# A new order for the first three blocks of a conditioned sequence kernel, with one activation table set

## What is computed

```python
x = _L0_cond_ref(x, theta, phi)            # rotate channel pairs by theta and phi of the sample
# L1
h = _noise_encoding(t, E)                  # sines and cosines of 5000 * t * freqs
h = silu(h @ W1 + b1)
h = h @ W2 + b2
scale = (h @ Wsc + bsc)[:, None, :]
shift = (h @ Wsh + bsh)[:, None, :]
out = silu(scale * _layer_norm(x, gamma, beta) + shift)     # mean and variance over a whole sample
out = out @ W_in + b_in
out = silu(scale * _layer_norm(out, gamma, beta) + shift)
out = out @ W_out + b_out
x = out + x
# L2: U and V (512 x 32) are orthogonalised by Gram-Schmidt, and a steering term of rank 32 is added
# L3: a transformer block (16 heads, causal), gated per sample
```

## Time and profile before

| what | value |
|---|---|
| median of 3 runs | 1610.24 us (1608.3 to 1611.57) |
| span of the profiled execution | 1610.9 us; its own time is not given apart from the span, which is 0.66 us above the median |
| TensorE busy | 1585.8 us (98%), weight loads 1299.5 us (81%) |
| VectorE, ScalarE, GpSimd busy | 1166.6, 982.8, 410.9 us |
| DMA | 254.79 MB, 158 GB/s on average |

### The profile page before, as it was taken

One profiled execution on the slowest core, in us unless ns is written; L12 is line 12 of the kernel. 1 busy time (PEld: TensorE's weight loads), 2 busy tenths in 40 slices (PEclk: granted clock), 3 DMA queues, 4 the chain that ended last, 5 costly groups with the idle time before them and its releaser, 6 DMA issues.

```text
span 1610.9 us, 27177 instructions
## 1 busy us (share of the span) xinstructions
PE 1585.8 (98%) x9296; PEld 1299.5 (81%) x9298; DVE 1166.6 (72%) x2767; ACT 982.8 (61%) x2331; POOL 410.9 (26%) x605
## 2 busy tenths in 40 slices
PE   7999999999999999999999999999999999999999
PEld 4688786777777777777777688898999999999998
DVE  7999888786969686868778576785655656565643
ACT  6888766887878787878778755352433324242422
POOL 8998810313222313131312110201010110202010
PEclk8999999999999999999999999999999999999999
DMA  7042135543545444444337435866464555556361
GB/s 308 0 183 97 66 126 126 149 130 92 138 95 139 100 115 122 111 116 115 88 90 214 167 152 207 303 262 232 178 234 170 213 225 188 212 178 265 142 211 68
DMA packets 62257, 254.79 MB, mean 158 GB/s; under 512 B 10628, under 2 KB 16004, under 8 KB 46760
## 3 DMA queue, kind: packets, MB, share of 16 engines
q1 hardware_dynamic: 62120, 253.06, 48.2%
HBM read 153.93 MB, written 48.23 MB: 125 GB/s over the span
## 4 chain that ended last, share of the span: by engine, by line
PE 90%; POOL 3%; DMA 2%; DVE 2%; ACT 1%; issue 1%; SPq 1%; POOLq 0%; DVEq 0%; ACTq 0%
PE psum L83 24%; PE psum L84 23%; PE psum L85 23%; PE psum L1529 5%; PE psum L1549 5%; PE psum L1579 4%; PE psum L1470 1%; DMA k_weights<-w_factors 1%; PE psum L1478 1%; PE psum L2451 1%; DMA k_raw<-in_t_w 1%; POOL k_gs_square L252 1%; POOL k_gs_root L247 1%; ACT psum L1229 1%; POOL k_gs_scaled L256 1%
## 5 line engine op out<-in xcount | busy, mean ns | idle before, releaser
L1229 ACT ACTIVATE psum<-psum,b_mx 128x512 f32<-128x512 f32 (+3 forms) x512 | 258.9, 509 | 63.2 <-DVE b_mx L990 62.0
L990 DVE CUSTOM_DVE_ANT_0 psum<-psum,b_mask 128x512 f32<-128x512 f32 (+3 forms) x512 | 244.7, 506 | 53.0 <-PE psum L1529 48.1
L2398 ACT ACTIVATE k_act<-k_stack_f,k_smalls 128x512 f32<-128x512 f32 x112 | 80.9, 722 | 303.6 <-DVE k_stack_f L2237 297.1
L1241 ACT ACTIVATE k_exps<-psum 128x512 f32<-128x512 f32 (+1 forms) x384 | 194.6, 532 | 59.4 <-PE psum L1549 58.1
L864 POOL TENSOR_SCALAR_AFFINE_SELECT k_exps<-k_exps 128x256 f32<-128x256 f32 x256 | 96.4, 413 | 381.0 <-ACT k_exps L1241 379.1
L2097 POOL TENSOR_SCALAR k_result<-k_result,k_pb 128x512 f32<-128x512 f32 x32 | 59.2, 1866 | 434.9 <-DVE k_result L2156 434.9
L2216 DVE TENSOR_TENSOR k_act_lo<-k_act,k_act_hi 128x512 fp32r<-128x512 f32 x112 | 77.2, 690 | 120.6 <-ACT k_act_hi L2401 120.6
L83 PE MATMUL psum<-k_act_hi,k_w_hi 128*128 128x512 f32 x384 | 150.8, 393 | 0.0
L84 PE MATMUL psum<-k_act_lo,k_w_hi 128*128 128x512 f32 x384 | 150.5, 392 | 0.0
L85 PE MATMUL psum<-k_act_hi,k_w_lo 128*128 128x512 f32 x384 | 150.2, 391 | 0.0
L2237 DVE TENSOR_TENSOR k_raw<-psum,k_raw 128x256 f32<-128x256 f32 x168 | 70.5, 421 | 106.0 <-PE psum L85 95.4
(11 more groups left out here) (372 smaller groups left out, 4418.2 us busy)
## 6 DMA issues: line engine op xcount, KB each, us to landing
k_stack<-w_factors SPq DMA_DIRECT2D x35, 1792.0 KB, 7.7
k_stack<-k_samples SPq DMA_DIRECT2D x384, 128.0 KB, 2.4
k_weights<-w_factors SPq DMA_DIRECT2D x17, 1792.0 KB, 7.5
x<-k_tokens SPq DMA_DIRECT2D x10, 1024.0 KB, 4.3
k_tokens<-x SPq DMA_DIRECT2D x8, 1024.0 KB, 5.1
d<-k_result SPq DMA_DIRECT2D x32, 256.0 KB, 2.9
k_raw<-x SPq DMA_DIRECT2D x8, 1024.0 KB, 4.8
k_raw<-d SPq DMA_DIRECT2D x8, 1024.0 KB, 7.1
```

What stands on the lines that cost most here:

```text
L990: last = dve.tensor_tensor_reduce(got, got, mask[:, S - width:S], -INV_SQRT_DH, -2.0 * MASKED, ALU.add, ALU.min, mx[n % 2][:, h, t:t + 1])
L1229: act.activation(sc(n, u)[:, at:at + width], sc(n, u)[:, at:at + width], ACT.Exp, bias=mx[n % 2][:, h, t:t + 1], scale=-1.0, accum_out=sum ...
L1241: act.activation(exps[n % 2][:, h, at:at + width], by_key(n, u)[:, 0:width], ACT.Exp, scale=INV_SQRT_DH).then_inc(k_act, 1)
L2398: act.activation(act_f[:], whole_tile, ACT.Gelu, bias=small(smalls, "b1", 2 * pair % M + second)).then_inc(pair_gelu, 1)
```

## The change

The order of four engines' lists is changed in the opening, up to block 2, and from there on everything is as before.

- SyncE: W_in's first half is loaded behind the four weights of the modulation, gamma's and beta's first halves ahead of it, then the second halves of gamma, beta and W_in. The number of loads is the same.
- ScalarE: a new step `tables` names the set that holds both silu and sine. `weight_high(0, 0)` goes behind `squares(1)`, `weight_high(0, 1)` between the silus of block 0, the crosses of sample 2 and three of the four `bias` steps of block 0 go behind silus of block 1.
- VectorE: `hidden_biased` goes ahead of `rotate(1, 1)`; `spread`, `mean(1)`, `modulated`, `weight_low` and the `low` steps of blocks 0 and 1 change places with `centre` and `gs_step`.
- TensorE: the counts and places of `hold` change; `layer_columns(0)` comes right behind `mean(0)`; block 0 runs four openings and then four closings, where it ran three, three, one and one. Behind `opening(1, 0)` and `mean(2)` the order is the old one.
- GpSimd's list is not changed.

```diff
--- before.py
+++ after.py
@@ -464,6 +464,9 @@
                 ins = act.activation(h1[:, j, 0:B], t_bank(0)[:, j * B:(j + 1) * B], ACT.Silu, bias=small(smalls, "t_b1", j))
             ins.then_inc(mlp_act, 1)
 
+        def tables():
+            act.preload_act_table_set("silu_and_others")
+
         def rows_out(k):
             act.wait_ge(t_full, (2, 4)[k])
             act.activation(spread_out[k], t_bank(1 + k), ACT.Copy).then_inc(mlp_act, 1)
@@ -476,7 +479,7 @@
                 act.wait_ge(wout_ld, 16)
             act.activation(whole(w_hi[k])[:, at], flat(raw)[:, at], ACT.Copy).then_inc(w_hi_set, 1)
 
-        return steps(sines_out, hidden_out, rows_out, weight_high, crosses, squares, silu_high, bias)
+        return steps(tables, sines_out, hidden_out, rows_out, weight_high, crosses, squares, silu_high, bias)
 
     def tensor(pe):
         def mean(n):
@@ -2618,18 +2621,18 @@
 
     mod.gs_in()
     mod.smalls_in()
-    mod.w_in_in(0)
     mod.x_in(0)
     mod.layer_in(0)
     mod.x_in(1)
     mod.layer_in(1)
     mod.layer_in(2)
+    mod.layer_in(3)
     mod.gamma_in(0)
-    mod.layer_in(3)
+    mod.beta_in(0)
+    mod.w_in_in(0)
+    mod.gamma_in(1)
+    mod.beta_in(1)
     mod.w_in_in(1)
-    mod.gamma_in(1)
-    mod.beta_in(0)
-    mod.beta_in(1)
     mod.x_in(2)
     mod.w_out_in()
     mod.x_in(3)
@@ -2808,41 +2811,41 @@
     mod.gs_step(1)
     mod.rotate(0, 0)
     mod.rotate(0, 1)
-    mod.weight_low(0, 0)
     mod.rotate(1, 0)
     mod.mean(0)
+    mod.hidden_biased()
     mod.rotate(1, 1)
     mod.gs_step(1)
-    mod.hidden_biased()
+    mod.spread(0)
+    mod.mean(1)
     mod.centre(0, 0)
-    mod.spread(0)
     mod.shift_rows_out()
-    mod.gs_step(1)
-    mod.mean(1)
-    mod.centre(0, 1)
     mod.modulated(0)
     mod.shift(0, 0)
     mod.modulated(1)
-    mod.centre(1, 0)
+    mod.gs_step(1)
+    mod.centre(0, 1)
+    mod.weight_low(0, 0)
+    mod.spread(1)
+    mod.low(0, 0)
     mod.shift(0, 1)
     mod.weight_low(0, 1)
-    mod.spread(1)
-    mod.low(0, 0)
     mod.gs_step(1)
+    mod.centre(1, 0)
+    mod.low(0, 1)
     mod.centre(1, 1)
-    mod.low(0, 1)
     mod.shift(1, 0)
     mod.shift(1, 1)
+    mod.low(1, 0)
     mod.rotate(2, 0)
     mod.gs_step(1)
     att.row_high()
+    mod.low(1, 1)
     mod.rotate(2, 1)
-    mod.low(1, 0)
     mod.gs_step(1)
     att.row_low()
     mod.mean(2)
     mod.weight_low(1, 0)
-    mod.low(1, 1)
     mod.centre(2, 0)
     mod.spread(2)
     mod.gs_step(1)
@@ -3371,8 +3374,8 @@
 
 def scalar_head(mod, att):
 
+    mod.tables()
     mod.sines_out()
-    mod.weight_high(0, 0)
     mod.crosses(0, 0)
     mod.hidden_out()
     mod.crosses(0, 1)
@@ -3381,20 +3384,23 @@
     mod.rows_out(0)
     mod.squares(0)
     mod.rows_out(1)
+    mod.squares(1)
+    mod.weight_high(0, 0)
+    mod.silu_high(0, 0)
+    mod.silu_high(0, 1)
     mod.weight_high(0, 1)
-    mod.squares(1)
-    for k in range(4):
-        mod.silu_high(0, k)
+    mod.silu_high(0, 2)
+    mod.silu_high(0, 3)
     mod.weight_high(1, 0)
+    mod.silu_high(1, 0)
+    mod.silu_high(1, 1)
+    mod.bias(0, 0)
     mod.crosses(2, 0)
+    mod.silu_high(1, 2)
+    mod.silu_high(1, 3)
     mod.crosses(2, 1)
-    mod.silu_high(1, 0)
-    mod.bias(0, 0)
-    mod.silu_high(1, 1)
-    mod.silu_high(1, 2)
     for k in range(1, 4):
         mod.bias(0, k)
-    mod.silu_high(1, 3)
     mod.squares(2)
     mod.weight_high(1, 1)
     att.safety_out()
@@ -3819,29 +3825,28 @@
 
     mod.hold(6, 1)
     mod.gs_products()
+    mod.hold(8, 1)
+    mod.first_layer()
+    mod.hold(10, 1)
+    mod.layer_rows(0)
+    mod.hold(2, 1)
+    mod.mean(0)
+    mod.layer_columns(0)
+    mod.hold(3, 1)
+    mod.layer_rows(1)
+    mod.variance(0)
+    mod.layer_rows(2)
+    mod.mean(1)
     mod.hold(4, 1)
-    mod.first_layer()
-    mod.hold(2, 1)
-    mod.layer_rows(0)
-    mod.mean(0)
-    mod.hold(6, 1)
-    mod.layer_columns(0)
-    mod.variance(0)
-    mod.layer_rows(1)
-    mod.layer_rows(2)
-    mod.hold(4, 1)
-    mod.mean(1)
     mod.layer_columns(1)
     mod.layer_columns(2)
+    mod.hold(6, 1)
+    mod.variance(1)
     mod.hold(16, 1)
-    mod.variance(1)
-    mod.hold(6, 1)
-    for k in range(3):
+    for k in range(4):
         mod.opening(0, k)
-    for k in range(3):
+    for k in range(4):
         mod.closing(0, k)
-    mod.opening(0, 3)
-    mod.closing(0, 3)
     mod.opening(1, 0)
     mod.mean(2)
     mod.opening(1, 1)
```

## The result

| | before | after |
|---|---|---|
| median | 1610.24 us (7 runs, 1608.3 to 1614.93) | 1616.45 us (7 runs, 1613.31 to 1618.43) |
| ratio, 95% interval | | 1.0041 [1.0028, 1.0054] |
| span of the profiled execution | 1610.9 us | 1614.6 us (its own time 1616.28, 1.7 more) |
| TensorE, VectorE, ScalarE, GpSimd busy | 1585.8, 1166.6, 982.8, 410.9 us | 1586.4, 1167.5, 981.3, 404.6 us |

The account below looks back on a forecast made before the run. TensorE was taken to bound the kernel, with 90% of the last chain; the opening's lead, lost in block 1, left `closing(1, 0)` at 52.9 against 49.92, so +3.0 us on 1610.24 gave 1613.2 us, range 1607.0 to 1617.0.

Parts of the forecast that it names:

- A: Whole kernel: the summed lag of +3.0 us reaches the end, 1612.2 to 1615.0 us; chance 0.50.
- B: TensorE's wait before `mean(2)`: the clock falls there, costing up to 2.6 us more, 1614 to 1616 us; chance 0.14.
- part 3: Opening: more products on the constant tile keep TensorE's clock at 2.4 GHz; a low clock would add up to 1.9 us.
- column 4 at the slow pace: Block 0: GpSimd's column 4 as slow as before, ending at 32.3 us in place of 30.9; adds 1.4 us.
- C: Behind the opening: idle time up to 250 to 285 us takes up the lag, 1608.5 to 1612 us; chance 0.24.
- Parts 1 and 3: Opening: loads W_in's first half stood before land 1.24 us sooner, W2's at 14.0; more holds keep the clock high.
- Part 2: ScalarE's opening: one table set saves a load of 1.28 us, worth nothing because `layer_rows(0)` waits for W2.
- Part 4: Small products of the opening: `layer_columns(0)` at 15.7 us, first silu at 24.3, 3.2 us sooner.
- Part 5: Block 0: first large product at 28.5 us against 32.20, a lead of 3.7 us; column 4 taken as 30.9.
- Part 6: Block 1: lead lost waiting for biases, then VectorE's `mean(2)`; `variance(2)` at 52.7 us, `closing(1, 0)` 52.9 against 49.92.
- D: GpSimd's columns: less stretching by VectorE cuts waits, the sum falls to about 0, 1605.5 to 1610 us; chance 0.09.
- The step that failed: From profiled span to median: 3.0 us on the span of 1610.9 taken as 3.0 on the median of 1610.24.

Follow-up runs that it names:

- old_loads: The kernel after with SyncE's load list as before (W_in's first half ahead of the modulation's weights); 1619.14 us, ratio 1.005.
- fewer_holds: The kernel after with 4 and 2 products on the constant tile around the first layer in place of 8 and 10; 1613.66 us, ratio 1.0027.
- table_only: The kernel before with only the one table set loaded first; 1611.64 us, ratio 1.0006.
- biases_first: The kernel after with ScalarE's block-1 list alone back in the old order, VectorE's left new; 1615.96 us, ratio 1.0039.
- mean2_first: The kernel after with VectorE's `mean(2)` moved ahead of the Gram-Schmidt step and `row_low`; 1615.04 us, ratio 1.0033.
- warm_wait: The kernel after with 24 products on the constant tile between `opening(1, 0)` and `mean(2)`; 1614.97 us, ratio 1.0034.
- before_again: The kernel before, unchanged, measured and profiled a second time; 1610.06 us, ratio 0.9994.
- old_block1: The kernel after with ScalarE's and VectorE's block-1 lists back in the old order; 1612.17 us, ratio 1.0014.
- lists_b: The kernel after's loads, holds and table set, with the lists of blocks 0 to 3 in another order than lists_a; 1612.73 us, ratio 1.0018.
- lists_a: The kernel after's loads, holds and table set, lists of blocks 0 to 3 reordered: Gram-Schmidt steps spread, biases earlier, `row_low` behind `mean(3)`; 1611.51 us, ratio 1.0007.
- only_block1: The kernel before with only ScalarE's and VectorE's block-1 lists in the new order; 1614.58 us, ratio 1.0035.

## Why the prediction was right, and where it was not

The direction, the range and the mechanism held; the size did not, and that the range held is partly luck. The measured 6.2 us is twice the sum of 3.0, above A (up to 1615.0) and above B (up to 1616). It lies within the bound of +6.3 only because that bound holds 1.9 us for a low clock in part 3 and 1.4 for column 4 at the slow pace, and neither came. The prediction had a slower kernel at 0.38 and no difference at 0.47. Its 0.15 for a faster one leans on "some of C", whose own range begins at 1608.5, above the 1607.0 it is meant to undercut.

**Parts 1 and 3.** W2's product was put at 14.0 and came at 13.65; the granted clock was 1.00 as said. The traces of old_loads and fewer_holds show both as real, though in old_loads the load and the clock act together. **Part 2** was nothing, and nothing it was (table_only). **Part 4**: 15.7 said, 15.44 seen; the first silu 24.3 and 24.52. **Part 5**: the first large product 28.5 and 28.67. Column 4 was taken to end at 30.9 and its reader ran at 31.13. **Part 6**: `opening(1, 0)` 40.6 and 40.75; `mean(2)` on TensorE 47.2 after 5.2 us of standing, 47.43 after 5.03; VectorE's `mean(2)` 50.4 and 50.70; `variance(2)` 52.7 and 53.05. A chain of operations in fixed lists could be added up to 0.4 us over 50 us, from the durations of the trace before alone. The two waits behind each other that Part 6 names are those that biases_first and mean2_first pull apart.

**Rival B** was right in its condition and wrong in its price. 5.03 us of standing do lower the clock, to 0.50, and nine of the twelve products of the openings follow at 0.43 us as said; "what follows at 1.2 GHz costs the difference" did not come, for the products are at full pace again from 51.83, before the squares end. That is by a hair: the openings end at 52.83, the squares at 52.90. mean2_first, biases_first and warm_wait show when B would have been the case: where the squares are done sooner (49.73), or where the wait stands in front of `variance(2)` and the low clock behind it.

**Rival C** fell for the most part. Of the 3.40 us at `variance(2)` 1.0 was taken up before 100 us, 0.37 of it in a wait at 76.43 that before has and after has not. At the loose place of 250 to 285 us the lag is 2.45 us at its first row (260.13 against 257.68 for the same product); the idle time there is 3.77 us instead of 3.43, and the trace of before has a clock of 0.95 where after has 1.00, so the half microsecond of lag that goes there does not show that idle time took it up. **D** fell in block 1, where it mattered: the L256 of column 4 took 1.96 us instead of 3.16, but the reader of column 6 still waited 0.92 us, as before. The Trainium skill (SBUF — State Buffer, on the shared port pair) has a GpSimd operation that reads SBUF blocked whole by a VectorE operation with two SBUF inputs that began first; the trace agrees in that the 64-partition L256 took 1.96 us here beside such work and 0.42 us at 7.26 us beside small operations.

**The step that failed** is the last: "a difference of 3.0 on the one is 3.0 on the other". The two profiled executions differ by 3.7 us (1614.6 - 1610.9), close to the sum of 3.0, and what is over it is in the lag at the end: 1.3 us more than at 209 us, with 0.94 and 0.3 us more of waits for weight loads at 1054.80 and 1040.51 us (from 100 to 209 us it is handed on whole, as said, but not to the end). But the medians differ by 6.2. The 70 later executions of the kernel before have a median span of 1608.6 us, and only 10 of them reach the 1610.9 of the profiled one. The seven of the kernel after have a median span of 1614.6, which is that of its profiled one. So the sum was made against an execution that was some 2.3 us slow for its kernel: 3.7 + 2.3 = 6.0, about the 6.2. Its median of 1610.24 hid this, since a time is 1.7 us or more above its span (1616.28 and 1614.6 in after): an execution that spans 1610.9 took about 1612.6.

Where the profiled execution of before lost its 2.3 us is shown in part only. The fall of the clock behind 809.53 us costs it 1.5 us against six other executions; but after's has that fall too, so it does not explain the difference of the two. Part of the rest may be the opening: table_only, whose own time lies at its median (1611.51 and 1611.64), is 1.10 us ahead of it at block 3, and before_again, 4.8 us above its median, is 2.68 us behind; neither makes up the whole.

**What stays open.** The new weight wait near 1054 us (0.5 to 1.1 us) is in both executions of after, in old_block1, biases_first, mean2_first, warm_wait, lists_b and old_loads, and in none of the four with the old opening; fewer_holds and lists_a have the new opening and not the wait. old_loads excludes the order of loads as its cause. What else ties it to the opening was not found. Of old_block1's 2.4 us over before (1.0014) the trace shows none at block 3; its traced execution lost 4 us between 829 us and the end, most of it to waits for loads (1.92 us at 866.78 for `k_maxima`, 2.19 at 1040.72 for `k_weights`). With 1616.05 us it was the slowest of the eleven, 3.9 above their median, so these waits need not be in the others.

## What to carry to other kernels

Where every engine works down a list in order, a lead in an opening is worth what it still is at the first instruction that collects from all engines; look for that instruction (here `mean(2)`, behind four biases) and count, for every engine, what the new list puts in front of it. If two engines' chains end there within a microsecond, moving one of them back moves the wait and not the time. Look also at what the wait does to the clock, and where the low clock then falls: ahead of an operation for which TensorE must wait anyway it is hidden, behind that operation it is paid. And compare a sum of a few microseconds with more than one profiled execution, each held against the median of its own kernel, before it is carried from a span to a median.

## What the runs showed of the hardware

- The same opening does not run alike each time. In three executions with the old loads and holds (before, before_again, table_only) the first large product came at 32.20, 34.89 and 31.13 us. In before_again the first layer's load ended TensorE's wait at 10.93 and the clock was below full for part of 20.2 to 32.2 us; with after's opening, two executions gave 28.67 and 29.43.
- Waits of 5.03 us (after), 2.84 (old_block1), 2.61 (only_block1) and 2.40 (warm_wait, in front of `variance(2)`) were each followed by products at the granted clock of 0.50, 0.43 us apart. The wait of 1.37 us in front of `variance(2)` in before was not (0.23 apart). A wait of 1.1 us near 810 us was followed by a clock of 0.50 to 0.66 in eight executions and of 1.00 in six; the fall cost 1.5 us.
- The low clock cost 1.2 to 2.6 us where it fell on TensorE's own chain (warm_wait, biases_first) and nothing where another engine's chain ended later (after).
- A weight load of 1792 KB, whose median from issue to landing is 7.6 us in the kernel after, was waited for 0.5, 0.8, 2.2 and 2.6 us in the same place near 1040 us by kernels that differ only within the first 80 us. It took 13.0 us from issue to landing in before, 13.4 in after, 15.2 in lists_a and 15.3 in table_only.
